# A small power on GpSimd between neighbouring indirect transfers, in a two-layer transformer with expert routing

## The reference, cut to what matters

```python
x = layernorm(x + attention_0(x))          # causal
x = layernorm(x + experts_0(x))            # 8 experts, the best 2 for each token
x = layernorm(x + attention_1(x))          # not causal, with biases
x = layernorm(x + experts_1(x))            # 15 experts, the best 3, and a shared expert

def experts_0(x):
    gates, idx = top_k(softmax(x @ gate_w + gate_b), 2)
    h = relu(x @ w1[e] + b1[e])            # for each expert e
    return sum over the chosen e of gate_e * (h @ w2[e] + b2[e])
```

## Time and profile before

| | us |
|---|---|
| timed, median of 3 runs | 944.91 (943.97 to 946.92) |
| profiled execution, span from its first to its last instruction | 1048.6 |
| profiled execution, its own time | not listed |
| GpSimd busy in the profiled execution | 429.6, 41% of the span |
| scatters, 160 | 159.6 busy |
| gathers, 160 | 154.7 busy |

### The profile page before, as it was taken

The page is one execution under the profiler, slowest core; times in us unless marked ns, Lnnn a source line. Parts: engine busy times, 40 slices in busy tenths (PEclk is TensorE's granted clock), DMA queues, the critical chain, the costliest instruction groups (busy, mean ns, idle before and its releaser), DMA issues.

```text
span 1048.6 us, 23098 instructions
## 1 busy us (share of the span) xinstructions
PE 808.7 (77%) x7666; PEld 537.5 (51%) x7666; DVE 657.8 (63%) x1916; ACT 500.0 (48%) x971; POOL 429.6 (41%) x654
## 2 busy tenths in 40 slices
PE   4789878779896878779888797777877795877750
PEld 3456555546664655446545453443444684756640
DVE  2867757666543776767478676786744442565674
ACT  2255545555463565636766465674544252223310
POOL 3002332322144455642354544635366304555565
PEclk9678989989998899888989987987757898899885
DMA  5875866776647551673655543323030387766533
GB/s 122 182 203 149 180 166 178 174 206 157 160 124 147 115 122 44 137 207 109 154 132 122 134 110 75 93 52 72 23 105 33 119 258 242 208 180 188 160 88 83
DMA packets 118772, 144.51 MB, mean 138 GB/s; under 512 B 13155, under 2 KB 92673, under 8 KB 118657
## 3 DMA queue, kind: packets, MB, share of 16 engines
q1 hardware_dynamic: 106689, 121.27, 45.9%
q0 software_dynamic: 10240, 20.99, 7.2%
q10 hardware_dynamic: 1728, 0.79, 0.3%
HBM read 89.78 MB, written 54.41 MB: 138 GB/s over the span
## 4 chain that ended last, share of the span: by engine, by line
PE 26%; DVE 13%; issue 11%; another core or an unknown queue 8%; ACT 4%; DMA 4%; POOL 3%; ACTq 1%; SPq 0%; POOLq 0%; DVEq 0%
DVE mp L1383 4%; PE bank_O L1207 3%; PE bank_FH L1289 3%; PE bank_N L1301 3%; PE pair_T L1188 3%; DMA G<-yd,ypos 2%; ACT P L1021 2%; PE pair_S L1166 2%; PE pair_T L1301 2%; POOL xs L945 1%; DVE X L1588 1%; POOL G L959 1%; PE bank_O L1289 1%; PE bank_M L1127 1%
## 5 line engine op out<-in xcount | busy, mean ns | idle before, releaser
L1383 DVE TENSOR_REDUCE mp<-pair_S 128x4 f32<-128x1024 f32 (+1 forms) x248 | 270.7, 1092 | 149.4 <-PE pair_S L1166 106.0
L1021 ACT ACTIVATE P<-pair_T 128x768 f32<-128x768 f32 (+1 forms) x256 | 234.6, 916 | 122.7 <-PE pair_T L1188 82.6
L959 POOL DMA_INDIRECT G<-yd,ypos x160 | 154.7, 967 | 144.5 <-DMA yd<-yb 57.2
L945 POOL DMA_INDIRECT xs<-X,ypos x160 | 159.6, 997 | 91.9 <-DVE ypos L1535 44.4
L1207 PE MATMUL bank_O<-P,V 128*18 128x256 f32 (+1 forms) x2048 | 131.4, 402 | 2.8 <-issue 2.3
L1188 PE MATMUL pair_T<-QK 51*128 51x256 bf16 (+1 forms) x1024 | 105.9, 282 | 35.3 <-ACT P L1021 27.3
L1166 PE MATMUL pair_S<-QK 48*128 48x256 bf16 (+1 forms) x992 | 101.4, 282 | 20.8 <-DVE mp L1383 12.4
L904 POOL TENSOR_TENSOR rstd<-mv,half 128x2 f32<-128x2 f32 x48 | 9.7, 201 | 213.6 <-DVE mv L1432 211.9
L1207 PEld LDWEIGHTS bank_O<-P,V 128*18 128x18 f32 x2048 | 59.2, 107 | 55.9 <-issue 31.4
L1188 PEld LDWEIGHTS pair_T<-QK 51*128 51x128 bf16 x1024 | 49.1, 100 | 66.7 <-ACT P L1021 38.3
L1150 PE MATMUL pair_T<-bmat 64*128 64x128 bf16 (+1 forms) x544 | 50.9, 265 | 25.2 <-ACT P L1021 20.2
(11 more groups left out here) (172 smaller groups left out, 1437.2 us busy)
## 6 DMA issues: line engine op xcount, KB each, us to landing
QK<-wtab SPq DMA_DIRECT2D x62, 257.0 KB
W<-w_in SPq DMA_DIRECT2D x46, 321.0 KB
yd<-yb SPq DMA_DIRECT2D x53, 256.0 KB
stk<-parts SPq DMA_DIRECT2D x32, 384.0 KB
QK<-stk SPq DMA_DIRECT2D x64, 192.0 KB
xs<-zeros SPq DMA_DIRECT2D x19, 512.0 KB, 5.7
xp<-xs SPq DMA_DIRECT2D x33, 256.0 KB
QK<-stk SPq DMA_DIRECT2D x64, 128.0 KB
```

Of the source, the lines that this page charges most:

```text
L945: pool.indirect_dma_start(xs[g % 2][0:reach(a) * PAGE], bass.IndirectOffsetOnAxis(ypos[L][:, 2 * b + blk, k:k + 1], 0), X[:, 2 * b + blk, ...
L959: pool.indirect_dma_start(G[i][:, blk, k, :], None, yd[g][0:reach(q) * PAGE], bass.IndirectOffsetOnAxis(ypos[L][:, 2 * b + blk, k:k + 1], 0))\
L1021: act.activation(P[:, i:i + 2, 0:n], pair["T"][:, :].rearrange("p (h c) -> p h c", h=2)[:, :, 0:n], ACT.Exp, scale=SCALE)\
L1383: dve.tensor_reduce(mp[:, a % 2, 0:n, :, 0, p].rearrange("p a r -> p r a"), S, AX.X, ALU.max, negate=True)\
```

## The change

Between two neighbouring indirect transfers of GpSimd's list it puts a power of 128x2 elements, written to a tile that nothing reads. Its inputs are constant. Each of these powers first waits for the one before it. A pair counts when each of the two steps is a scatter of either layer or a gather of layer 0. That holds at 156 places: behind 49 scatters of layer 0, 68 scatters of layer 1 and 39 gathers of layer 0. The order of all other steps is the same. An image of layer 0 has four scatters in a row as a rule, thus three such places; one of layer 1 has six, thus up to five.

```diff
--- before.py
+++ after.py
@@ -478,6 +478,12 @@
 PLAN = plan()
 
 
+POOL_STEPS = ("residual_bias", "inverse_std", "route_diff", "route_pos_mul", "scatter", "gather")
+ON_POOL = [(name, x) for name, x in PLAN if name in POOL_STEPS]
+PAUSES = [step for step, after in zip(ON_POOL, ON_POOL[1:])
+          if all(name == "scatter" or name == "gather" and x[0] < NB for name, x in (step, after))]
+
+
 def run_plan(ops):
     for name, x in PLAN:
         if name in ops:
@@ -570,6 +576,7 @@
         bvb = sb("bvb", [D, D])
         warm = sb("warm", [D, 1])
         half = sb("half", [D, 2, 2])
+        idle = sb("idle", [D, 2])
 
         qk_words = QK[:, :, :, :, :].bitcast(F32).rearrange("p a s h t -> p (a s h t)")
         w_words = W[:, :, :].rearrange("p i c -> p (i c)")
@@ -703,6 +710,8 @@
         sh_added = signal("sh_added")
         out_stored = signal("out_stored")
 
+        paused = signal("paused")
+
         def last_norm(k, q):
 
             return k == 1 and q >= NB
@@ -920,6 +929,13 @@
                 pool.tensor_tensor(dm[L][:, b % 4, :, n:n + k], m8[:, a % 4, :, 0:k], top.broadcast_to((D, 2, k)), ALU.subtract)\
                     .then_inc(diffed.sem, 1)
 
+            def pause(step):
+                if step in PAUSES:
+                    i = PAUSES.index(step)
+                    if i:
+                        pool.wait_ge(paused.sem, i)
+                    pool.tensor_tensor(idle[:, :], half[:, 1, :], half[:, 0, :], ALU.pow).then_inc(paused.sem, 1)
+
             def route_pos_mul(a):
                 L = a // NB
                 n, k = EXPERTS[L], TOPK[L]
@@ -944,6 +960,7 @@
                 pool.wait_ge(normed[0].sem, normed[0].all(a))
                 pool.indirect_dma_start(xs[g % 2][0:reach(a) * PAGE], bass.IndirectOffsetOnAxis(ypos[L][:, 2 * b + blk, k:k + 1], 0),
                                         X[:, 2 * b + blk, :], None).then_inc(scattered[g].sem, DMA)
+                pause(("scatter", (a, blk, k)))
 
             def gather(q, blk, k):
                 L, b = q // NB, q % NB
@@ -959,6 +976,7 @@
                 pool.indirect_dma_start(G[i][:, blk, k, :], None, yd[g][0:reach(q) * PAGE],
                                         bass.IndirectOffsetOnAxis(ypos[L][:, 2 * b + blk, k:k + 1], 0))\
                     .then_inc(gathered[L][i][blk].sem, DMA)
+                pause(("gather", (q, blk, k)))
 
             run_plan({"residual_bias": residual_bias, "inverse_std": inverse_std,
                       "route_diff": route_diff, "route_pos_mul": route_pos_mul, "scatter": scatter, "gather": gather})
```

## The result

The change makes the kernel slower: 1016.7 us (1010.8 to 1020.5, 4 runs) against 945.9, ratio 1.073 with the interval 1.068 to 1.078. That is 71 us where 17 were forecast; the direction was right, the size was off by a factor of four.

A forecast was written before the change was run, and what follows sets the result against it. GpSimd, idle more than half the time, was taken to set the pace only before the switch after layer 1's attention. End of attention 7.5 plus middle 9.4 gave +16.9 us on 944.9, thus 962 us; range 950 to 984.

The forecast's parts named there:

- The price of a pause: Between two indirect transfers on GpSimd: 1.94 us end to end in place of 1.26, taken as 0.67 us per pause.
- What lies on the path: the middle: Gather and scatter runs at five places, plus one scatter at 796.71 us: 14 pauses of 0.67 us on the chain, +9.4 us.
- the count of 14 pauses on the chain: Pauses in runs of indirect transfers on the first trace's last-ending chain, from image 0's gathers to 796.71 us; +9.4 us.
- a chain gets longer by what is put in it: Middle term: a chain released step by step grows by the added pauses, 14 x 0.67 = +9.4 us.
- The end of attention: Layer 1's last scatters, before the first page load: positions 4.1 us later plus five pauses of 3.4 us, +7.5 us.
- the carried lag: Through GpSimd's instructions: plus 0.67 us per pause, minus GpSimd's waits for other engines, never below zero, other engines' times fixed.
- GpSimd becomes the bound of the last images: Rival: 22 pauses at 770 to 826 us unabsorbed, 14.7 us, and ScalarE's waits 18 us; +33, 978 us; chance 0.17.
- Only the tail: Rival: in the middle other work waits beside the chain, so only the end of attention counts; +7.5, 952 us; chance 0.16.
- no cost: Rival: transfers queue in the DMA engines or powers fit the 0.30 us gap; within 0.3% of 944.9; chance 0.10.
- relief of the DMA queues: Rival: spacing lets gathers on the chain land sooner, saving 13.3 us and another 17; 932 us; chance 0.07.
- VectorE beside GpSimd: VectorE's combining operations slowed by meeting more powers on GpSimd: 0 in the sum, 3 us in the range.

The follow-up runs named there:

- The early pauses: Only the 29 pauses of the scatters of images 0 to 9, added to the kernel before: 943.3 us, ratio 0.999.
- the middle: Only the 92 pauses from image 10's scatters to layer 0's last gather, added to the kernel before: 996.4 us, ratio 1.057.
- the tail: Only the 35 pauses of the scatters of images 23 to 31 behind layer 0's last gather, added to the kernel before: 963.5 us, ratio 1.024.

## Why the prediction was wrong, step by step

**The price of a pause was right:** 0.71 us against 0.67 (the terms that the forecast adds give 1.94 - 1.26 = 0.68). GpSimd's busy time came to 555.8 us against 550 forecast. The last scatter lands 2.3 us after its start as before, VectorE's wait for it grew from 7.5 to 11.1 us, and the stretch behind it has its old length (189 us to the end in place of 188). The early pauses are free as forecast, with the cover that was named, and the loss is where the chain was said to run.

**"What lies on the path: the middle" was mis-sized: 9.4 us against 51.** Two things in it failed.

The first is the count of 14 pauses on the chain (one of them, at 796.71 us, lies in the tail). It came from a trace that was 104 us longer than a timed run. I saw this and wrote that GpSimd catches up in the stalls, but let it change neither the sum nor much of the range. In the trace without stalls the chain holds 56 paused transfers, middle and tail together, in place of 22: 56 x 0.71 = 40 us. That count, an estimate by the forecast's own method, would have given 985 us.

The second is "a chain gets longer by what is put in it". That is the least that it gets longer. As GpSimd falls behind, the chain moves onto it. After the change 78 pauses stand on the chain (50 in the middle, 28 in the tail), 78 x 0.71 = 55 us of the 71. That count is the least, too: the profile follows this chain back to 380 us only, and 23 pauses of the middle lie ahead of that. GpSimd is about 5 us late there.

**"The end of attention" was mis-sized too: 7.5 us against 18 (23 by the ratio).** The step that failed is the carried lag, "other engines' times held fixed" and "minus whatever time GpSimd waited for another engine". With a clean trace the same carrying gives 13.0 us at the last scatter, so the stalls account for about 5 of the missing us, and the rest is the method: for the whole kernel it gives 13 where the last scatter is 72.5 us late. By this method the lag vanishes wherever GpSimd waits for longer than it is late, for instance before image 23, in the wait of 6.46 us that is shown above. It does not vanish there: the wait is 6.49 us long in the changed kernel and begins 52 us later. residual_bias waits there until TensorE has transposed the normalised X. ScalarE had normalised it 7 us before, so the transposes came when TensorE's own list reached them, and that list was 52 us late as a whole. Nothing but GpSimd's work was changed in the program, so what made it late leads back to GpSimd: earlier waits for a normalised X, a gather or a route_diff, as they grew in the rows above, and perhaps the clock that is named below. Which of them did it can't be read at this place. A wait of this kind moves along with the lag. Only where what GpSimd waits for comes no later, as at 278.6 us, does the lag go. The stretches above say the same in sum: in 434 to 651 us GpSimd still idles 82 us of 217, and yet 27 of its 38 added us are lost.

**The rivals.** "GpSimd becomes the bound of the last images" came nearest, in kind (its added waits of ScalarE are there, 28 us against the 18 that it priced) and in the sign of the error; its price was 33 us. "Only the tail", "no cost" and "relief of the DMA queues" are refuted: the first by the middle's 51 us, the last two by the result itself and by the run with the powers behind the transfers, where the spacing is as before and the time is not. The small cost that I allowed for VectorE beside GpSimd (3 us in the range) doesn't show: its busy time is 654 us in place of 653.

**What stays open.** 55 of the 71 us are pauses on the chain behind 380 us, and some 5 us were lost ahead of it; how the rest divides isn't settled. One candidate was not tested apart: TensorE's granted clock fell from 0.909 of full speed in the mean to 0.878, and its busy time for the same instructions rose from 761.7 to 797.0 us. Whether the extra 35 us of matmul lie on the path, no run here separates, but the runs give a size. One execution of the kernel before had a clock of 0.891 and took 952.7 us, one with the powers behind the run had 0.892 and took 1002.5: 50 us more at the same clock. And over 46 executions of the kernel before on one chip (0.891 to 0.924) the time is 3 to 4 us longer for each 0.01 of clock that is missing. By that the four executions of the changed kernel, at 0.874 in the mean in place of 0.907, would be some 10 to 13 us longer; that is an estimate, and it takes all of that relation for the clock's doing.

## What to carry to other kernels

Before a forecast rests on a chain, compare the profiled span with the timed runs; where they differ by a tenth, take a second profile, since a chain from a stalled execution hides the engine that is late.
An idle of an in-order engine is slack only if what it waits for doesn't depend on that engine's own earlier results; in a pipeline that comes back to the engine several times for each image, price added work at most of its full length wherever the loop is closed, here 0.6 to 0.9 us for each us (71 for the 111 us of all powers, 51 to 54 for the middle's 65, 18 to 23 for the tail's 25), and at nothing only where the work runs open, as before the first gather.
Forecast added delay and removed delay apart: 0.1 us more at a time cost its share, 0.20 us less at a time gave nothing.

## What the runs showed that was not expected

Two profiled executions of the same kernel had spans of 1048.6 and 942.4 us with timed runs of 945 us both times. In the longer one VectorE and ScalarE had single waits of up to 9.8 and 6.6 us with no releaser in the trace; the second has none.

A short operation between two indirect transfers costs more than its own time less the gap that it could fill: the gap before the next transfer shrinks only from 0.30 to 0.19 us, and that transfer takes 1.03 in place of 0.96 us.
